# Attention scores of the next pair issued one K unit earlier on TensorE, with maximum and exponential moved along

## The reference

```python
q = query @ Wq + bq
kv = context @ Wkv + bkv                      # k and v, 16 heads x 32
scores = einsum('bhid,bhjd->bhij', q, k) * SCALE
attn = softmax(scores, axis=-1)
out = einsum('bhij,bhjd->bhid', attn, v)
```

## Time and profile before

| | us |
|---|---|
| median of 3 runs | 2648.12 |
| lowest and highest of the 3 | 2643.91 and 2648.58 |
| profiled execution, first to last instruction (span) | 2643.8 |
| its TensorE busy time | 2413.4 (91%) |
| its mean granted TensorE clock | 0.965 of 2.4 GHz |

### The profile page before, as it was taken

How to read it: one execution, slowest core, us unless ns; L and a number is a source line. 1 busy time by engine, 2 the same in 40 slices (tenths; PEclk the granted TensorE clock), 3 DMA queues, 4 the chain that set the end, 5 groups by cost and what they waited for, 6 DMA issues and landing times. The chain is left out here.

```text
span 2643.8 us, 41258 instructions
## 1 busy us (share of the span) xinstructions
PE 2413.4 (91%) x14596; PEld 2125.1 (80%) x14596; DVE 1749.9 (66%) x2316; ACT 1099.2 (42%) x1878; POOL 1081.5 (41%) x436
## 2 busy tenths in 40 slices
PE   8899999999999999999999999998579928999994
PEld 6688888888888888888888888886438628999993
DVE  3177777777778787777777777778764425554552
ACT  3244444444444454444444444444322214444440
POOL 2155555555455554545545555554320021111113
PEclk9999999999999999999999999999889959999997
DMA  4211111111111111111111111113030033443433
GB/s 149 90 29 45 37 45 41 54 43 38 38 49 43 35 57 37 38 52 33 53 45 37 39 46 54 39 42 102 8 142 1 1 123 136 148 157 141 167 123 119
DMA packets 114016, 176.91 MB, mean 67 GB/s; under 512 B 51856, under 2 KB 71568, under 8 KB 113808
## 3 DMA queue, kind: packets, MB, share of 16 engines
q1 hardware_dynamic: 108048, 159.51, 19.2%
q0 software_dynamic: 2560, 8.39, 1.0%
q10 hardware_dynamic: 3200, 6.29, 0.6%
HBM read 137.19 MB, written 36.96 MB: 66 GB/s over the span
## 5 line engine op out<-in xcount | busy, mean ns | idle before, releaser
L356 POOL TENSOR_TENSOR k_parts<-k_t,k_parts 64x1602 fp32r<-64x1602 f32 x128 | 426.0, 3328 | 458.1 <-DVE k_parts L418 458.0
L646 PE MATMUL ps_kv<-ctx_hi,wk_hi 128*128 128x256 f32 (+1 forms) x1536 | 464.0, 302 | 13.0 <-POOL ctx_lo L345 13.0
L646 PE MATMUL ps_kv<-ctx_lo,wk_hi 128*128 128x256 f32 (+1 forms) x1536 | 441.1, 287 | 0.0
L646 PE MATMUL ps_kv<-ctx_hi,wk_lo 128*128 128x256 f32 (+1 forms) x1536 | 440.6, 287 | 0.0
L370 POOL TENSOR_TENSOR v_parts<-v,v_parts 128x832 fp32r<-128x832 f32 x128 | 281.4, 2199 | 381.1 <-ACT v_parts L581 379.9
L451 DVE TENSOR_SCALAR probs_both<-probs_both,row_inv 128x1601 f32<-128x1601 f32 x128 | 407.4, 3183 | 4.5
L646 PE MATMUL ps_kv<-wv_hi,ctx_hi 128*128 128x512 f32 (+1 forms) x832 | 340.1, 409 | 0.0
L646 PE MATMUL ps_kv<-wv_hi,ctx_lo 128*128 128x512 f32 (+1 forms) x832 | 327.8, 394 | 0.0
L646 PE MATMUL ps_kv<-wv_lo,ctx_hi 128*128 128x512 f32 (+1 forms) x832 | 326.7, 393 | 0.0
L551 ACT ACTIVATE k_t<-ps_kv,bk_sb 128x256 f32<-128x256 f32 (+1 forms) x384 | 185.8, 484 | 306.3 <-PE ps_kv L646 301.7
L458 DVE TENSOR_TENSOR probs_t<-ps_pt,probs_t 128x512 fp32r<-128x512 f32 x368 | 205.9, 559 | 153.7 <-ACT probs_t L563 150.4
(11 more groups left out here) (215 smaller groups left out, 4219.2 us busy)
## 6 DMA issues: line engine op xcount, KB each, us to landing
w_raw<-w_dram SPq DMA_DIRECT2D x96, 512.0 KB, 4.8
ctx_raw<-ctx_dram SPq DMA_DIRECT2D x81, 512.0 KB, 3.6
rows_in<-zeros SPq DMA_DIRECT2D x90, 128.0 KB, 2.0
ctx_raw<-ctx_dram SPq DMA_DIRECT2D x16, 644.0 KB, 4.2
q_blocks<-q_parts SPq DMA_DIRECT2D x256, 32.0 KB, 1.8
rows_out<-zeros SPq DMA_DIRECT2D x1, 6144.0 KB, 21.2
rows<-rows_in SPq DMA_DIRECT2D x8, 768.0 KB, 5.7
rows_out<-down ACTq DMA_DIRECT2D x8, 768.0 KB, 3.6
```

The source lines that it names most:

```text
L356: nc.gpsimd.tensor_tensor(k_parts[64 - 64 * s:128 - 64 * s, :], k_t[par][64 * s:64 * s + 64, g, :], k_parts[64 * s:64 * s + 64, :].bitcast ...
L646: last = nc.tensor.matmul(o, still, moving, start=(k == 0 and i == 0), stop=(k == DT - 1 and i == 2))
```

## The change

Three things move, and nothing is added or taken away. On PE, `scores` of the next pair moves from behind `turn` 2 to behind `turn` 1, in front of gap 1's K unit. On DVE, `guard` of the next pair moves in front of `rest` 2. On ACT, `exponent` of the next pair moves in front of `copy_group` 3. The waits of each step are as they were.

```diff
@@ -471,9 +471,9 @@
                     rest(n, 1, kv)
-                    rest(n, 2, kv)
                     if one_on:
                         guard(n + 1, one_on[2])
+                    rest(n, 2, kv)
                     rest(n, 3, kv)
@@ -587,7 +587,7 @@
-                        if g == NG - 1 and later(b, par, p, 1):
+                        if g == NG - 2 and later(b, par, p, 1):
                             exponent(n + 1, (p + 1) % PAIRS)
@@ -704,10 +704,10 @@
                     turn(n, p % 2, 1, kv)
+                    if one_on:
+                        scores(one_on[0], one_on[2])
                     beside(1)
                     turn(n, p % 2, 2, kv)
-                    if one_on:
-                        scores(one_on[0], one_on[2])
                     turn(n, p % 2, 3, kv)
```

## The result

| | before | after |
|---|---|---|
| median us (runs) | 2646.02 (4) | 2835.53 (4) |
| lowest to highest | 2643.91 to 2648.58 | 2832.94 to 2844.12 |
| ratio, 95% interval | | 1.0717 (1.0699 to 1.0736) |
| span of the profiled execution | 2643.8 | 2834.3 |

The account below looks back on a forecast made before the run. PE was taken to bound the loop; 179 us for 15 batches, 9 for the last batch and 5 for the clock make 193, giving about 2841 us as a median, 7.3% slower, range 2812 to 2885.

Parts of the forecast that it names:

- the scores covered the chain: Between `turn` 2 and `turn` 3: scores hid the 2.00 us chain through `ps_pt`; moving them leaves a 1.65 us hole per pair.
- The maximum is out of the way in ordinary pairs: On DVE: the maximum, now in front of `rest` 2, is done 0.6 us before it is missed.
- Pair 7: Last pair of each batch: `rest` 2 behind the maximum makes a 2.90 us hole ahead of `turn` 3; net +1.9 us.
- Won at `turn` 0: Ahead of `turn` 0: the waits for the normalise go, -1.5 us a batch.
- list of signs: Signs expected in the changed profile, among them `split_k` on DVE ending about 1 us after the exponential.
- A batch: Each of 15 batches with units: 7 x 1.65 + 1.9 - 1.5 = 11.95 us more, +179 us in all.
- The clock: PE's clock behind pair 7's longer pauses: 5 us lost in all, bounds 0 and 22; 1.00 in the loop.
- The last batch: Batch without units: no hole, but `split_k`, POOL, normalise and `turn` 0 come later behind the exponential; +9 us.
- The faster one: Rival: the chain from `turn` 2 to `turn` 3 costs nothing, for instance with its own bank; 2607 us, 3 in 100.
- the third rival: Rival: the chain over POOL and the normalise becomes the bound, `turn` 0 waiting; 2900 us or a little more, 8 in 100.
- the margin: Ahead of `turn` 0: after the change the normalise is done 0.5 us before PE needs it.
- The clock rival: Rival: the clock falls behind the holes, 1.5 us each; 3020 us, or 2900 behind one in three; 7 in 100.

Follow-up runs that it names:

- e4: The changed kernel with `turn` 3 writing bank `ps_o` instead of `ps_pt` and waiting for `rest` 1; 2714.1 us, ratio 1.0247.
- e5: e4 with the exponential back behind the rounding of group 3, scores and maximum still early; 2603.5 us, ratio 0.9832.
- e1: The kernel before with PE's move alone, DVE and ACT in the old order, `turn` 3 in `ps_pt`; 2820.2 us, ratio 1.0644.
- e6: The kernel before with `turn` 3 in `ps_o` and nothing else changed; 2642.9 us, ratio 0.9983.
- e3: The changed kernel with ACT's part undone (exponential back behind the rounding of group 3), `turn` 3 in `ps_pt`; 2826.4 us, ratio 1.0683.
- e2: The kernel before with DVE's and ACT's moves alone, PE in the old order, `turn` 3 in `ps_pt`; 3143.6 us, ratio 1.1868.
- e8: e1 with `turn` 3 in `ps_o`, DVE and ACT in the old order; 2788.5 us, ratio 1.0520.

## Why the prediction was right, point by point

**PE bounds the loop; the scores covered the chain.** Right in the main. With the same chain and no cover, PE idles 1.40 us and `turn` 3 starts 2.00 us after `turn` 2, to the hundredth what was read off the kernel before. e4 and e5 take away the shared bank, and in e4's groups the pause is 0.0; e1 has it with PE's move alone. Two readings of the kernel before were not quite right. That PE's own pieces, 0.35 and 1.65, also make 2.00 proved nothing, since the 1.65 was read up to the start of `turn` 3, which the chain had set: the scores take 1.62 (e6). And PE was not alone in setting the pace: in pairs 2, 3, 4 and 6 of every batch `turn` 0 started 0.06 us behind the end of the normalise, so that the chain through POOL and the normalise was as long as PE's work there. Where such a wait was some 0.2 us or less it is no pause in the earlier trace rows, because the matmul in front had not ended yet.

**The maximum is out of the way in ordinary pairs.** Right: 0.56 us to spare, 0.6 worked out.

**Pair 7**: counted from `turn` 1, `turn` 3 was to start at 7.38 us and started at 7.20 (1119.21 - 1112.01); `turn` 2 was to start at 4.13 and started at 4.26, since the scores began 0.79 behind `turn` 1 instead of 0.60. The hole, less the 0.35 of `turn` 2, is 2.59 where 2.90 was forecast. The mechanism is as told: POOL holds the scores for 0.19 us, and `rest` 2 stands behind the maximum (1.81) and its negative. e1, where it doesn't, has no pause over 1.4.

**Won at `turn` 0.** The waits for the normalise went, as forecast; the loop has none left. Their worth was more than the 1.5 us a batch. From `turn` 1 to the next `turn` 1, pairs without a fall of the clock grew by 1.57, 1.40, 0.96, 0.72, 1.61, 1.38 and 1.63 us (pairs 0 to 6), 9.3 together where seven holes of 1.65 make 11.55: so 2.3 us were won (0.2 of them the wait of 0.03 us a pair that e6 shows). The step from pair 7 grew by 1.74, where 1.9 was forecast. In the ordinary pair above, `split_k` ends at 1029.78, 1.6 us behind the exponential's 1028.20; that is what the prediction's sum gives (7.5 - 5.95), while its list of signs has "about 1 us".

**A batch** cost 11.9, as the forecast 11.95, but this includes the clock, which I had put in a term of its own; without it, it is 11.0. **The clock** fell to 1.2 GHz 8 times in the loop, 5 times at pair 7's pause (twice in its last 0.5 us, three times within 1.3 us of its end) and 3 times in the first pair after the loop jumps back, where the pause ahead of `turn` 3 was 2.0 to 2.5 us; never behind one of 1.40. That other place I had not seen. These longer pauses, and pair 7's, are why PE idles 182.8 us ahead of `turn` 3 in all, where 165 to 175 was to be the sign, and the granted clock is 0.99 and not 1.00 in 260 to 1820 us. The fall behind the pause shown above:

```profile
1119.70:1123.10 3.40, 3.40 (x10) 2.66 (x9) 2.58 (x4) 0.69 (x3) 1.15 (x1) 0.50 0.03 5
```

Batches with such a fall are about 1.6 us longer (124.3 against 122.75 from maximum to maximum), 13 us in all where 5 were taken and 22 was the bound. So two errors met: the pairs were cheaper than forecast by 0.9 us a batch (14 in all), the clock was 8 us dearer. That the total came out within 3 us is partly luck.

**The last batch** cost 11.7 us, 9 forecast. The mechanism is as told: `rest` 3 starts at 2007.06, behind the exponential's end at 2006.78, and with ACT's part undone (e3) 8.7 of the 11.7 are gone.

**The total** was 193 forecast and 190.5 measured on the profiled executions; 2841 against 2835.5 as a median. Of the difference, 2 us are the median of before, which came out lower with a fourth run. Of the 4.3 us between span and median, 1.8 are no spread: every run's time lies 1.8 us over its span (2836.04 and 2834.3 for the changed kernel).

**The rivals.** The faster one had half of its condition right, "a bank of its own": e5, at 2603.5 us where the rival gave 2607, has that bank, but also the exponential back in its old place. The kernel that the rival described is e4, with the bank and all three moves, and it took 2714: there the third rival (the chain over POOL and the normalise) comes true and costs 111 us. So the sentence of the prediction that with two banks this change would end near the first rival's time was wrong: the pause went, but the time came down that far only when the exponential went back (e5). In the changed kernel itself the third rival did not come true, and the margin, 0.5 us by the sum, held: `turn` 0 starts 0.3 to 0.4 us behind the normalise's end in pair 4, 0.5 to 0.6 in pair 3 and 0.9 or more in the others. The clock rival was wrong for pauses of 1.4 us and right for those of 2.74 (e2).

The rule of the Trainium skill, Perfetto Trace Analysis, Optimizing Tensor Performance, Matmuls, on rotating independent groups through PSUM banks is borne out here by e3 against e5: 223 us between two kernels that differ only in the bank of one small group. It says nothing of e6, where another bank gave 0.2%: with the scores between the two groups, the bank was late by only 0.03 us.

## What to carry to other kernels

Before work is moved ahead on the bounding engine, ask what it was covering where it stood: two groups that share a PSUM bank need the length of the emptying chain between them (here 2.00 us), whatever fills it. A cover that fits to the hundredth is a warning: here the work behind it was already waiting, by 0.03 us. And an early result is only worth having if the engines that must handle it reach it early without pushing back something more urgent: here the maximum could go ahead (185 us, e8 and e5), the exponential could not (111 us, e4 and e5).

## What the runs showed of the hardware that was not expected

How often TensorE's clock fell to 1.2 GHz at a pause ahead of `turn` 3 rose with the pause's length, and not in proportion. Counted in the traces over the batches with units, from 145 us to their end: at 118 pauses of 1.4 us in e1 there was no fall, and none at 99 in the changed kernel; of its 13 pauses of 2.34 to 2.36 us, 5 had one, and of the six of 1.6 to 2.5 us behind the loop's jump, 3; in e3 there was none at 99 pauses of 1.4, 3 at 13 of 2.32 to 2.36 and 3 at the six behind the jump; in e2, 109 of 119 pauses of 2.7 us had one. I had allowed e2 up to 60 us for this. Length is not shown to be the only cause: e2's pauses come in every pair and pair 7's once in a batch, and the scores stand in front of the one, transposes in front of the other.

After such a fall a matmul of 512 columns took 0.63 us instead of 0.40. The V unit behind `turn` 3 takes 3.04 us at full clock (median of the 120 in the kernel before). In e2, 110 of its 120 took longer, 4.49 in the median, and the 120 together took 162 us more than at full clock. So a fall cost some 1.4 us, half of the pause of 2.74 over again, and all of the 158.6 us by which e2 lay over 2985 is there.
